# Causal attention in a four-part block: probability transposes, values and output projection each one step later, with four probability buffers

## The chip, the core and the metric

The kernel runs on one core of one Trainium2 chip. The metric is the device time of one execution in microseconds (us). The core has five engines that work side by side and wait for each other only through semaphores: TensorE (PE in the rows; its weight loads are PEld), VectorE (DVE), ScalarE (ACT), GpSimd (POOL) and SyncE (SP), which issues the transfers. Each engine runs its own instructions in their order.

## What is computed

The reference runs four stages on x of shape (4, 256, 256): windowed attention, a quantized feed-forward, a selective scan, and then a block of causal attention followed by a mixture of 32 experts. The change lies in the causal attention alone, which is this part of the reference (here 4 sequences of 256 positions, 32 query heads, 4 key and value heads of width 128):

```python
q = (h @ Wq).reshape(B, S, NH, HD)
k = (h @ Wk).reshape(B, S, KVH, HD)
v = (h @ Wv).reshape(B, S, KVH, HD)
q = _rope(q, pos)
k = _rope(k, pos)
...
scores = jnp.einsum('bqhd,bkhd->bhqk', q, k) / jnp.sqrt(jnp.float32(HD))
scores = jnp.where(causal[None, None], scores, jnp.float32(-1000000000.0))
attn = jax.nn.softmax(scores, axis=-1)
o = jnp.einsum('bhqk,bkhd->bqhd', attn, v).reshape(B, S, NH * HD) @ Wo
x = resid + o
```

## The kernel before

Five functions run one after the other: `windowed_attention`, `quantized_ffn`, `selective_scan`, `causal_attention`, `experts`. In `causal_attention` the outermost loop runs over the 4 groups of heads `g` (one key and value head, 8 query heads each), inside it over the 4 sequences `b`, and inside that over the 8 heads of the group. One **step** `n` is one head of one sequence, so a group has 32 steps and the stage 128. A **batch** in this text is the 8 steps of one `(g, b)`, and `r = n % 8` is a step's place in it. All precise products are three matmuls on a high and a low part (`product`, lines 73 to 75).

One head s goes through these pieces of work, each on several engines:

- `scores`: PE multiplies q and k into one of two PSUM banks (`SCOREB[s % 2]`, lines 1534 and 73 to 75). It waits for `exp_done` of head s-2, which has used that bank.
- `peak`: DVE adds the mask (line 1428) and takes two row maxima (line 1432).
- `softmax`: ACT takes the exponential (line 1318), DVE inverts the sums (`rden`, line 1443), POOL multiplies `prob` by them (line 1372) and signals `p_normed`.
- `turn_probs`: PE transposes `prob` in three pieces (line 1544), ACT copies the result (`pt_1`, `pt_h`, lines 1324 and 1325), DVE makes the low part `pt_l` (line 1438) and signals `p_lo`. PE's transpose of head s waits for `p_normed` of s and for `p_lo` of s-1, since there is one bank for it.
- `values`: PE multiplies with v (lines 73 to 75 and 1554), ACT copies `ot_h` (line 1329), DVE makes `ot_l` (line 1447).
- `project_out`: PE multiplies with the output weights (lines 73 to 75); after a batch's last head DVE adds the sum to `z` (line 1457).

Beside the heads, the next batch is prepared: `kv` and `q` project keys, values and queries (PE), rotate them (DVE lines 1389 and 1392, then POOL into `kr` and `qr`, lines 1365 and 1358), and `turn_k`, `turn_q` transpose them (PE lines 1524 and 1514, ACT lines 1301 to 1307, DVE lines 1416 and 1421). There is one `qr` buffer for each half of the positions, and POOL's `q(m, i)` waits until PE has turned all of head quartet m-1. During the first three groups `weights` splits the next group's weights in 9 pieces at every second step (ACT line 1290, POOL line 1342).

The order of all this work is written out by hand in `schedule`, and every engine walks the same list and does its own part of each entry. `yield "scores", *at(1)` in step n means the scores of head n+1. So in step n, before the change, PE does the scores of head n+1, the transposes of n-1, the values of n-2 and the projection of n-3. Steps 0 to 2 are written out, then a loop of three passes of 32 steps starts at step 3, and the last group is written out again.

A step in which PE does these four things alone is called **light** here; a step that also has a projection of q or kv is **heavy**.

Of the kernel before, what the change touches and what calls it, by code (L numbers as in the profile page):

```python
# [17 lines left out]
F32 = mybir.dt.float32  # L18
# [3 lines left out]
ALU = mybir.AluOpType  # L22
# [4 lines left out]
P = 128  # L27
# [1088 lines left out]
def causal_attention(core, z, ln1_w, weights_in, consts):  # L1116
# [10 lines left out]
    with scope:  # L1127
# [19 lines left out]
        v_1 = sb("v1_1", [P, 2, HD1], F32)  # L1147
        neg_max = sb("neg_max1", [P, 2, 2], F32)
        sums = sb("sums1", [P, 2, 2], F32)
        rden = sb("rden1", [P, 2, 2], F32)  # L1150
        prob = sb("prob1", [P, 2, BANDS], F32)
        pt_h, pt_l = (sb(f"pt1_{n}", [P, 2, S], F32R) for n in "hl")
        pt_1 = sb("pt1_1", [P, 2, P], F32)
        ot_h, ot_l = (sb(f"ot1_{n}", [P, 2, S], F32R) for n in "hl")
# [46 lines left out]
        def ahead(g, m):  # L1201
            return (g, m) if m < 2 * B else (g + 1, m - 2 * B)
# [15 lines left out]
        def schedule(g, first, end, last):  # L1218


            for n in range(first, end):
                at = lambda k: (g + (n + k) // STEPS, (n + k) % STEPS)
                own = not last or n < STEPS
                (gg, s), more = at(0), own and (not last or n // REP1 + 1 < B)
                b, r = s // REP1, s % REP1
                if own and (not last or n + 1 < STEPS):
                    yield "scores", *at(1)
                if own:
                    yield "softmax", *at(0)
                if own and (not last or n + 1 < STEPS):  # L1230
                    yield "peak", *at(1)
                if n >= 1 and (not last or n < STEPS + 1):
                    yield "turn_probs", *at(-1)
                if own and r in (1, 2):
                    yield "turn_q", gg, 2 * b + 1, r - 1
                if more and r == 4:
                    yield "turn_k", *ahead_b(gg, b + 1)
                if more and r in (5, 6):
                    yield "turn_q", *ahead(gg, 2 * b + 2), r - 5
                if n >= 2 and (not last or n < STEPS + 2):  # L1240
                    yield "values", *at(-2)
                if n >= 3:
                    yield "project_out", *at(-3)
                if more and r == 1:
                    yield "kv", *ahead_b(gg, b + 1)
                if more and r in (2, 3):
                    yield "q", *ahead(gg, 2 * b + 2), r - 2
                if more and r in (6, 7):
                    yield "q", *ahead(gg, 2 * b + 3), r - 6
                if not last and 6 <= s < 6 + 2 * PIECES and s % 2 == 0:  # L1250
                    yield "weights", gg + 1, (s - 6) // 2
# [4 lines left out]
        def run(eng, does):  # L1256


            def all_of(work):
                for kind, *what in work:  # L1260
                    if kind in does:
                        does[kind](*what)

            all_of([*FIRST, *schedule(0, 0, 3, False)])
            with eng.Fori(0, KVH1 - 1) as g:
                all_of(schedule(g, 3, STEPS + 3, False))
            all_of(schedule(KVH1 - 1, 3, STEPS + 3, True))

        with nc.Block() as block:
            @block.sync  # L1270
# [13 lines left out]
            def _(act):  # L1284
# [30 lines left out]
                def softmax(g, s):  # L1315
                    act.wait_ge(max_ready, STEPS * g + (s + 1))
                    for i, cols in enumerate((slice(0, P), slice(P, BANDS))):
                        act.activation(prob[:, s % 2, cols], psum[:, SCOREB[s % 2], cols], ACT.Exp,  # L1318
                                       bias=neg_max[:, s % 2, i:i + 1],
                                       accum_out=sums[:, s % 2, i:i + 1]).then_inc(exp_done, 1)  # L1320

# [12 lines left out]
            @block.gpsimd  # L1334
            def _(pool):
                def weights(g, piece):

                    hi, lo, raw, row, rows, cols = weight_piece(piece)
                    where = ds((g & 1) * raw.shape[1] + row, rows)
                    src = raw[:, row:row + rows, cols]  # L1340
                    pool.wait_ge(w_hi, PIECES * g + (piece + 1))
                    ins = pool.tensor_tensor(lo[:, where, cols], src, f(hi[:, where, cols]), ALU.subtract)
                    if piece in (2 * KD, PIECES - 1):
                        ins.then_inc(w_ready, 1)

                for piece in range(2):
                    weights(0, piece)
                norm.gpsimd(pool)
                for piece in range(2, PIECES):
                    weights(0, piece)  # L1350

                def q(g, m, i):
                    pool.wait_ge(parts, q_index(g, m, i) + 1)
                    before = turn_index(g, m - 1, 1) if m else k_turn_index(g, 0) - 1
                    if not known(before, 0):
                        pool.wait_ge(qk_turned, before + 1)
                    slot = q_index(0, m, i) % 2
                    pool.tensor_tensor(qr[:, i, :], part_a[:, slot, :], part_b[:, slot, :], ALU.add).then_inc(roped, 1)  # L1358

                def kv(g, b):  # L1360
                    index = kv_index(g, b)
                    pool.wait_ge(parts, index + 1)
                    slot = kv_index(0, b) % 2
                    cols = slice(0, 2 * HD1)
                    pool.tensor_tensor(kr[:].rearrange("p t n -> p (t n)"), part_a[:, slot, cols], part_b[:, slot, cols],
                                       ALU.add).then_inc(roped, 1)

                def softmax(g, s):
                    pool.wait_ge(rden_ready, STEPS * g + (s + 1))
                    for i, cols in enumerate((slice(0, P), slice(P, BANDS))):  # L1370
                        at = prob[:, s % 2, cols]
                        ins = pool.tensor_tensor(at, at, rden[:, s % 2, i:i + 1].to_broadcast([P, (i + 1) * P]), ALU.mult)  # L1372
                    ins.then_inc(p_normed, 1)

                run(pool, dict(q=q, kv=kv, softmax=softmax, weights=weights))

            @block.vector
            def _(dve):
# [61 lines left out]

                def softmax(g, s):
                    dve.wait_ge(exp_done, 2 * STEPS * g + (2 * s + 2 + 4))
                    dve.reciprocal(rden[:, s % 2, :], sums[:, s % 2, :]).then_inc(rden_ready, 1)  # L1443

                def values(g, s):
                    dve.wait_ge(o_hi, STEPS * g + (s + 1))
# [17 lines left out]
            def _(pe):  # L1464
# [75 lines left out]
                def turn_probs(g, s):  # L1540
                    pe.wait_ge(p_normed, STEPS * g + (s + 1))
                    pe.wait_ge(p_lo, STEPS * g + (s + 1))
                    for i in range(3):
                        ins = pe.transpose(psum[:, PTURNB, i * P:(i + 1) * P], prob[:, s % 2, i * P:(i + 1) * P],  # L1544
                                           core.ident[:])
                    ins.then_inc(p_turned, 1)

# [373 lines left out]
```

## Time and profile before

| | |
|---|---|
| time before, median of 3 runs | 1260.85 us (1260.09 to 1262.29) |
| profiled execution | 1260.24 us, of which its span is 1258.4 us |
| busy share of the span | PE 88%, DVE 68%, ACT 51%, POOL 50% |
| the causal attention in the span | about 478 to 954 us; heads from 492.6 us |
| in 490 to 954 us | PE busy 431.66 us, DVE 362.16, ACT 281.72, POOL 245.40; mean granted TensorE clock 0.99 |

The span is the time from the first to the last instruction in the trace. Times in rows are microseconds from its start. The granted clock is TensorE's clock as a share of 2.4 GHz, so 0.50 stands for 1.2 GHz. Matmuls are pipelined: the recorded length of one (0.28 us for 128x256) is longer than the distance to the next (0.12 us), so a recorded gap is shorter than the time that PE's queue stood still.

### The profile page before, as it was taken

To read this page: it belongs to the slowest core of one execution; us is meant where nothing else is said; L and a number is where in the kernel's file an instruction comes from. 1 tells how busy PE (TensorE), PEld (TensorE's weight loads), DVE (VectorE), ACT (ScalarE), POOL (GpSimd) and SP (SyncE) were. 2 spreads that over 40 slices of the span, in tenths; PEclk is the share of its full clock that TensorE was granted. 3 is DMA by queue.
4 is the path that set the end of the run, shared out by engine and by line. 5 is a ranking of instruction groups with operands and counts; after the bars stand their busy time and mean duration, and the time that the engine had idled before them with its cause. 6 is when DMAs were issued, how large, how long until landed. Compare 5 with 4: busy or idle time off the path is not lost. (4 is left out here: it accounts for less than half of the span.)

```text
span 1258.4 us, 22579 instructions
## 1 busy us (share of the span) xinstructions
PE 1105.8 (88%) x6776; PEld 916.0 (73%) x6776; DVE 856.1 (68%) x2126; ACT 637.7 (51%) x2027; POOL 623.7 (50%) x648
## 2 busy tenths in 40 slices
PE   5499989597579956999899999999997999999998
PEld 4366656386335525888888888888896888888887
DVE  4766785555388885878778777777886555555555
ACT  4356644122379942666566556655563434333332
POOL 3632361255277762565466446644442455555554
PEclk9699989588789977999999999999997999999999
DMA  8000000000212302002000200000001111111111
GB/s 231 1 1 1 0 0 1 10 1 11 69 67 84 126 11 76 2 2 77 3 1 2 77 3 2 1 2 2 1 2 28 50 50 43 44 50 50 38 50 46
DMA packets 43966, 41.35 MB, mean 33 GB/s; under 512 B 6161, under 2 KB 39985, under 8 KB 43873
## 3 DMA queue, kind: packets, MB, share of 16 engines
q1 hardware_dynamic: 42144, 39.02, 10.1%
q10 hardware_dynamic: 1728, 1.18, 0.3%
q8 instruction: 46, 0.75, 0.3%
q14 instruction: 48, 0.39, 0.1%
HBM read 39.08 MB, written 1.11 MB: 32 GB/s over the span
## 5 line engine op out<-in xcount | busy, mean ns | idle before, releaser
L1732 POOL TENSOR_TENSOR hid_l<-hid,hid_h 128x512 fp32r<-128x512 f32 x66 | 85.6, 1297 | 131.1 <-ACT hid_h L1701 131.1
L1358 POOL TENSOR_TENSOR qr<-r_part_a,r_part_b 128x512 f32<-128x512 f32 x64 | 82.4, 1287 | 125.1 <-DVE r_part_b L1392 123.8
L1372 POOL TENSOR_TENSOR prob<-prob,rden 128x128 f32<-128x128 f32 (+1 forms) x256 | 124.3, 509 | 37.5 <-DVE rden L1443 37.5
L1782 DVE TENSOR_TENSOR hid<-psum,silu 128x512 f32<-128x512 f32 x66 | 45.6, 691 | 129.3 <-ACT silu L1699 129.3
L1318 ACT ACTIVATE prob<-psum,neg_max 128x128 f32<-128x128 f32 (+1 forms) x256 | 106.0, 424 | 36.3 <-DVE neg_max L1432 31.4
L1774 DVE SCALAR_TENSOR_TENSOR x<-psum,weight,x 128x256 f32<-128x256 f32 x264 | 108.8, 475 | 0.0
L73 PE MATMUL psum<-xt_h,gu_l 128*128 128x512 f32 x264 | 105.5, 400 | 2.4 <-POOL gu_l L1717 2.4
L75 PE MATMUL psum<-xt_h,gu_h 128*128 128x512 f32 x264 | 104.5, 396 | 0.0
L74 PE MATMUL psum<-xt_l,gu_h 128*128 128x512 f32 x264 | 104.0, 394 | 0.0
L1699 ACT ACTIVATE silu<-psum 128x512 f32<-128x512 f32 x66 | 39.5, 598 | 117.6 <-PE psum L75 117.6
L913 POOL TENSOR_TENSOR drive<-u,b_all 128x1024 f32<-128x1024 f32 x32 | 76.3, 2387 | 40.1 <-DVE u L1007 20.2
L1324 ACT ACTIVATE pt<-psum 128x128 f32<-128x128 f32 x128 | 36.1, 282 | 115.1 <-PE psum L1544 114.7
L1544 PE MATMUL psum<-ident,prob 128*128 128x128 f32 x384 | 65.2, 279 | 25.8 <-POOL prob L1372 25.8
L1016 DVE TENSOR_TENSOR_SCAN h<-psum,drive 128x512 f32<-128x512 f32 x64 | 76.4, 1214 | 12.7 <-ACT psum L951 12.4
L73 PE MATMUL psum<-wo_h,ot_l 128*128 (+1 forms) x256 | 82.6, 323 | 0.2 <-DVE ot_l L1447 0.2
L1432 DVE TENSOR_REDUCE neg_max<-psum 128x1 f32<-128x128 f32 (+1 forms) x256 | 79.5, 352 | 4.4
L1389 DVE TENSOR_TENSOR r_part_a<-psum,rope 128x512 f32<-128x512 f32 (+1 forms) x80 | 50.7, 634 | 38.7 <-PE psum L75 38.6
L73 PE MATMUL psum<-wd_h,hid_l 128*128 128x256 f32 x264 | 74.7, 283 | 0.6 <-POOL hid_l L1732 0.6
L75 PE MATMUL psum<-wd_h,hid_h 128*128 128x256 f32 x264 | 74.7, 283 | 0.0
L74 PE MATMUL psum<-wd_l,hid_h 128*128 128x256 f32 x264 | 74.6, 282 | 0.0
L1087 PE MATMUL psum<-scaled,ident 128*128 128x512 f32 x128 | 70.9, 637 | 2.4
L74 PE MATMUL psum<-wo_l,ot_h 128*128 (+1 forms) x256 | 72.1, 282 | 0.0
(251 smaller groups left out, 3711.5 us busy)
## 6 DMA issues: line engine op xcount, KB each, us to landing
b_all<-scan_b_rows SPq DMA_DIRECT2D x16, 512.0 KB, 3.6
early<-in_L_ffn_Wq_dram SPq DMA_DIRECT2D x4, 1024.0 KB, 5.4
early<-in_L_ffn_Wo_dram SPq DMA_DIRECT2D x4, 1024.0 KB, 8.3
raw<-in_L_ffn_Wg_dram SPq DMA_DIRECT2D x32, 128.0 KB, 2.2
raw<-in_L_ffn_Wu_dram SPq DMA_DIRECT2D x32, 128.0 KB, 2.2
raw<-in_L_ffn_Wd_dram SPq DMA_DIRECT2D x32, 128.0 KB, 2.3
x<-_attn_hidden_states_dram SPq DMA_DIRECT2D x8, 128.0 KB, 4.6
early<-in_L_ffn_w_up_q_dram SPq DMA_DIRECT2D x1, 1024.0 KB, 6.3
```

Source lines behind the costliest of these rows:

```text
L73: pe.matmul(out, ll, rh, start=start, stop=False, skip_group_check=shared)
L74: pe.matmul(out, lh, rl, start=False, stop=False, skip_group_check=shared)
L75: return pe.matmul(out, lh, rh, start=False, stop=stop, skip_group_check=shared)
L913: pool.tensor_tensor(drive[:, k, :], u[:, k, :], b_all[:, n % BBUF, :], ALU.mult).then_inc(driven, 1)
L1016: dve.tensor_tensor_scan(h[:, k, cols], psum[:, DECAYB + i % 2, :], drive[:, k, cols], 0.0, ALU.mult, ALU.add).then_inc(scanned, 1)
L1087: pe.matmul(psum[:, YB[k] + half, :], core.ident[:], scaled[:, i % 4, :, :], start=n == 0, stop=n == NS - 1, skip_group_check=True).then_i ...
L1318: act.activation(prob[:, s % 2, cols], psum[:, SCOREB[s % 2], cols], ACT.Exp, bias=neg_max[:, s % 2, i:i + 1], accum_out=sums[:, s % 2, i: ...
L1358: pool.tensor_tensor(qr[:, i, :], part_a[:, slot, :], part_b[:, slot, :], ALU.add).then_inc(roped, 1)
L1372: ins = pool.tensor_tensor(at, at, rden[:, s % 2, i:i + 1].to_broadcast([P, (i + 1) * P]), ALU.mult)
L1432: ins = dve.tensor_reduce(neg_max[:, s % 2, i:i + 1], psum[:, SCOREB[s % 2], cols], AX.X, ALU.max, negate=True)
L1732: pool.tensor_tensor(hid_l[:, j, cols], hid[:, c, :], f(hid_h[:, j, cols]), ALU.subtract)\
L1774: dve.scalar_tensor_tensor(core.x[:, t, :], src, scale, core.x[:, t, :], ALU.mult, ALU.add)\
```

## The change

Three things are changed together. The transposes of a head's probabilities are done two steps behind its softmax entry instead of one, values three instead of two, and the output projection four instead of three; the preparation of keys, values and most queries moves one step later with them. `prob` and `rden` have four slots instead of two. The loop starts at step 4 instead of 3. The work itself is the same: each engine issues the same number of compute instructions.

```diff
-        rden = sb("rden1", [P, 2, 2], F32)
-        prob = sb("prob1", [P, 2, BANDS], F32)
+        rden = sb("rden1", [P, 4, 2], F32)
+        prob = sb("prob1", [P, 4, BANDS], F32)
...
-                if n >= 1 and (not last or n < STEPS + 1):
-                    yield "turn_probs", *at(-1)
+                if n >= 2 and (not last or n < STEPS + 2):
+                    yield "turn_probs", *at(-2)
                 if own and r in (1, 2):
                     yield "turn_q", gg, 2 * b + 1, r - 1
-                if more and r == 4:
+                if more and r == 5:
                     yield "turn_k", *ahead_b(gg, b + 1)
-                if more and r in (5, 6):
-                    yield "turn_q", *ahead(gg, 2 * b + 2), r - 5
-                if n >= 2 and (not last or n < STEPS + 2):
-                    yield "values", *at(-2)
-                if n >= 3:
-                    yield "project_out", *at(-3)
-                if more and r == 1:
+                if more and r in (6, 7):
+                    yield "turn_q", *ahead(gg, 2 * b + 2), r - 6
+                if n >= 3 and (not last or n < STEPS + 3):
+                    yield "values", *at(-3)
+                if n >= 4:
+                    yield "project_out", *at(-4)
+                if more and r == 2:
                     yield "kv", *ahead_b(gg, b + 1)
-                if more and r in (2, 3):
-                    yield "q", *ahead(gg, 2 * b + 2), r - 2
+                if more and r in (3, 4):
+                    yield "q", *ahead(gg, 2 * b + 2), r - 3
                 if more and r in (6, 7):
                     yield "q", *ahead(gg, 2 * b + 3), r - 6
...
-            all_of([*FIRST, *schedule(0, 0, 3, False)])
+            all_of([*FIRST, *schedule(0, 0, 4, False)])
             with eng.Fori(0, KVH1 - 1) as g:
-                all_of(schedule(g, 3, STEPS + 3, False))
-            all_of(schedule(KVH1 - 1, 3, STEPS + 3, True))
+                all_of(schedule(g, 4, STEPS + 4, False))
+            all_of(schedule(KVH1 - 1, 4, STEPS + 4, True))
```

The remaining edits replace `s % 2` by `s % 4` where `prob` and `rden` are indexed (ACT's exponential, POOL's multiplication, DVE's inversion, PE's transpose).

The first place is the last step of a batch on PE (r = 7), where `ident,prob` is the transpose of probabilities, `ident,qr` that of queries and `pt` the values. Before:

```order
L1534 MATMUL psum<-k_0,q_0 128x128
L73 MATMUL psum<-k_h,q_l 128x256
L74 MATMUL psum<-k_l,q_h 128x256
L75 MATMUL psum<-k_h,q_h 128x256
L1541 REGISTER_ALU
L1544 MATMUL psum<-ident,prob 128x128 x3
L73 MATMUL psum<-pt_h,v_l 128x256
```

Now:

```order
L1534 MATMUL psum<-k_0,q_0 128x128
L73 MATMUL psum<-k_h,q_l 128x256
L74 MATMUL psum<-k_l,q_h 128x256
L75 MATMUL psum<-k_h,q_h 128x256
L1541 REGISTER_ALU
L1544 MATMUL psum<-ident,prob 128x128 x3
L1514 MATMUL psum<-ident,qr 128x128 x4
L73 MATMUL psum<-pt_h,v_l 128x256
```

The query transpose has moved from r = 5 and 6 to r = 6 and 7, so it now stands in both steps that also project the next queries.

The second place is ACT's queue in a batch during which weights are split, around the copies of v (`v_1`, `v_h`); `wq_h<-early` is a weight piece. Before:

```order
L1310 REGISTER_ALU
L1312 ACTIVATE v_1<-psum 128x128
L1313 ACTIVATE v_h<-psum 128x128
L1316 REGISTER_ALU
L1318 ACTIVATE prob,sums<-psum,neg_max 128x128
L1318 ACTIVATE prob,sums<-psum,neg_max 128x256
L1324 ACTIVATE pt_1<-psum 128x128
```

Now:

```order
L1310 REGISTER_ALU
L1312 ACTIVATE v_1<-psum 128x128
L1313 ACTIVATE v_h<-psum 128x128
L1290 ISA
L1290 ACTIVATE wq_h<-early 128x512
L1316 REGISTER_ALU
L1318 ACTIVATE prob,sums<-psum,neg_max 128x128
L1318 ACTIVATE prob,sums<-psum,neg_max 128x256
```

The kv entry has moved from r = 1 to r = 2, an even step that can also hold a weight piece, so that piece now stands between the copy of v and the next exponential.

The third place is the beginning of the stage on PE, step 1 after its scores (`wkv` is the projection of keys and values). Before:

```order
L1544 MATMUL psum<-ident,prob 128x128 x3
L1514 MATMUL psum<-ident,qr 128x128 x4
L73 MATMUL psum<-wkv_h,xt_l 128x256
L74 MATMUL psum<-wkv_l,xt_h 128x256
L75 MATMUL psum<-wkv_h,xt_h 128x256
```

Now:

```order
L1514 MATMUL psum<-ident,qr 128x128 x4
L1534 MATMUL psum<-k_0,q_0 128x128
L73 MATMUL psum<-k_h,q_l 128x256
L74 MATMUL psum<-k_l,q_h 128x256
L75 MATMUL psum<-k_h,q_h 128x256
L1544 MATMUL psum<-ident,prob 128x128 x3
L1514 MATMUL psum<-ident,qr 128x128 x4
L73 MATMUL psum<-wkv_h,xt_l 128x256
```

Step 1 now holds only one query transpose after its scores; the first probability transpose and the kv projection follow behind the scores of step 2.

## Rows read from the trace of the kernel before

**Rows 1.** The page of the profile: its first line.

```profile
span 1258.4 us, 22579 instructions
```

**Rows 2.** Stretches: length, busy PE, PEld, DVE, ACT, POOL, granted clock, DMA, GB/s.

```profile
518.36:547.19 28.83, 27.21 (x207) 25.56 (x206) 22.79 (x70) 18.71 (x72) 18.38 (x25) 1.00 0.01 1
...
604.81:635.75 30.94, 27.33 (x208) 25.47 (x207) 23.05 (x70) 17.53 (x69) 13.43 (x21) 1.00 0.01 3
...
896.57:925.29 28.72, 27.01 (x208) 25.53 (x206) 22.81 (x70) 17.00 (x68) 13.43 (x21) 1.00 0.01 2
```

**Rows 3.** Waits of PE, 490 to 954 us: total us, times, longest.

```profile
PE psum L1544 <- POOL prob L1372: 25.8, 31, 1.0
```

**Rows 4.** Timeline, 842 to 847 us: start, length, instruction, idle before it and releaser.

```profile
842.88 0.69 DVE L1389 TENSOR_TENSOR r_part_a<-psum,rope 128x512 f32<-128x512 f32 x1 [0.53 <-PE psum L75]
...
844.15 0.15 DVE L1443 RECIPROCAL rden<-sums 128x2 f32<-128x2 f32 x1
...
844.31 1.30 POOL L1358 TENSOR_TENSOR qr<-r_part_a,r_part_b 128x512 f32<-128x512 f32 x1 [1.38 <-DVE r_part_b L1392]
...
844.89 0.38 PE L1534 MATMUL psum<-k,q 128*128 128x128 f32 x2
...
845.21 0.41 DVE L1438 TENSOR_TENSOR pt_l<-psum,pt_h 128x256 fp32r<-128x256 f32 x1
...
845.35 0.28 PE L75 MATMUL psum<-k_h,q_h 128*128 128x256 f32 x1
...
845.56 1.93 POOL L1372 TENSOR_TENSOR prob<-prob,rden 128x128 f32<-128x128 f32 x4
...
846.27 0.17 DVE L1443 RECIPROCAL rden<-sums 128x2 f32<-128x2 f32 x1 [0.32 <-ACT prob L1318]
...
846.60 0.55 PE L1544 MATMUL psum<-ident,prob 128*128 128x128 f32 x3 [0.97 <-POOL prob L1372]
```

**Rows 5.** Timeline of POOL, 681 to 685 us, and PE's wait behind it.

```profile
681.28 1.29 POOL L1358 TENSOR_TENSOR qr<-r_part_a,r_part_b 128x512 f32<-128x512 f32 x1 [2.23 <-DVE r_part_b L1392]
682.54 1.28 POOL L1342 TENSOR_TENSOR wo_l<-early,wo_h 128x512 f32 x1
683.78 0.97 POOL L1372 TENSOR_TENSOR prob<-prob,rden 128x128 f32<-128x128 f32 x2
```

**Rows 6.** Timeline of PE and DVE in the last batch's light steps, 939 to 943 us.

```profile
939.74 0.38 PE L1534 MATMUL psum<-k,q 128*128 128x128 f32 x2
940.61 0.41 DVE L1428 TENSOR_TENSOR psum<-psum,causal 128x256 f32<-128x256 f32 x1
941.94 0.38 PE L1534 MATMUL psum<-k,q 128*128 128x128 f32 x2
942.74 0.41 DVE L1428 TENSOR_TENSOR psum<-psum,causal 128x256 f32<-128x256 f32 x1
```

**Rows 7.** Timeline of a heavy step, 675 to 680 us.

```profile
675.61 0.38 PE L1534 MATMUL psum<-k,q 128*128 128x128 f32 x2
...
676.51 0.60 PE L1514 MATMUL psum<-ident,qr 128*128 128x128 f32 x4
...
678.14 0.70 ACT L1290 ACTIVATE wo_h<-early 128x512 f32 x1
...
679.63 0.38 PE L1534 MATMUL psum<-k,q 128*128 128x128 f32 x2
```

**Rows 8.** The start of the heads: timeline of PE and ACT.

```profile
496.22 0.46 PE L1534 MATMUL psum<-k,q 128*128 128x128 f32 x2 [2.31 <-ACT prob L1318]
...
498.01 0.20 ACT L1318 ACTIVATION_READ_ACCUMULATOR prob<-psum,neg_max 128x1 f32 x1
```

**Rows 9.** Busy time by stretch at the start of the heads.

```profile
491.40:498.10 6.70, 4.04 (x28) 3.41 (x27) 4.60 (x13) 1.72 (x8) 3.52 (x4) 1.00 0.00 0
498.10:501.50 3.40, 3.40 (x19) 3.40 (x18) 1.83 (x7) 1.62 (x9) 0.97 (x2) 0.52 0.00 0
```

**Rows 10.** The end of the stage: timeline of PE.

```profile
952.27 0.38 PE L73 MATMUL psum<-wo_h,ot_l 128*128 128x256 f32 x1 [0.23 <-DVE ot_l L1447]
```

More of the change, by code:

```diff
@@ L1317, in softmax @@
                     for i, cols in enumerate((slice(0, P), slice(P, BANDS))):
-                        act.activation(prob[:, s % 2, cols], psum[:, SCOREB[s % 2], cols], ACT.Exp,
+                        act.activation(prob[:, s % 4, cols], psum[:, SCOREB[s % 2], cols], ACT.Exp,
                                        bias=neg_max[:, s % 2, i:i + 1],
@@ L1370, in softmax @@
                     for i, cols in enumerate((slice(0, P), slice(P, BANDS))):
-                        at = prob[:, s % 2, cols]
-                        ins = pool.tensor_tensor(at, at, rden[:, s % 2, i:i + 1].to_broadcast([P, (i + 1) * P]), ALU.mult)
+                        at = prob[:, s % 4, cols]
+                        ins = pool.tensor_tensor(at, at, rden[:, s % 4, i:i + 1].to_broadcast([P, (i + 1) * P]), ALU.mult)
                     ins.then_inc(p_normed, 1)
@@ L1442, in softmax @@
                     dve.wait_ge(exp_done, 2 * STEPS * g + (2 * s + 2 + 4))
-                    dve.reciprocal(rden[:, s % 2, :], sums[:, s % 2, :]).then_inc(rden_ready, 1)
+                    dve.reciprocal(rden[:, s % 4, :], sums[:, s % 2, :]).then_inc(rden_ready, 1)
                 def values(g, s):
@@ L1543, in turn_probs @@
                     for i in range(3):
-                        ins = pe.transpose(psum[:, PTURNB, i * P:(i + 1) * P], prob[:, s % 2, i * P:(i + 1) * P],
+                        ins = pe.transpose(psum[:, PTURNB, i * P:(i + 1) * P], prob[:, s % 4, i * P:(i + 1) * P],
                                            core.ident[:])
```

## The prediction

> **What bounds the kernel now.** The kernel's span is 1258.4 us [rows 1], and the change touches only the causal attention, where the heads run from 492.6 to about 954 us. I read the stretches first: a batch of eight steps takes 28.83 us and PE is busy for 27.21 of it, DVE for 22.79, ACT for 18.71, POOL for 18.38, at a granted clock of 1.00 [rows 2]. The 14 batches between 518.36 and 925.29 us all look like the first and the last of these rows, except the two in which the loop jumps back (30.94 us is one). So PE sets the pace, its clock is full, and what can be won is the time in which its queue stands still.
>
> Then I read who PE waits for. Of its waits in the stage almost all are one kind: 31 times the transpose of probabilities (line 1544) waits for POOL's multiplication (line 1372), 25.8 us together, 0.83 us each [rows 3]. They are two per batch. The matmuls' recorded ends hide a part: the last scores matmul starts at 845.35, its successor would start 0.12 later at 845.47, and the transpose starts at 846.60 [rows 4]. That is 1.13 us of standing still where the row says 0.97, so each wait costs 0.16 more than its record: 0.99 us on average, 31 x 0.99 = 30.8 us in all.
>
> Why POOL is late is seen in the timeline. In [rows 4] DVE is held by the rotation of q and comes to its inversion at 844.15, POOL then adds `qr` (844.31 to 845.61) and only then multiplies two heads' probabilities in one run, 845.56 to 847.49, 0.97 us each; the first is done at about 846.54, and PE starts 0.06 later. In the other kind a weight piece of 1.28 us stands between `qr` and the multiplication [rows 5]. In both the multiplication comes about 1 us after PE wants it, following a heavy step.
>
> **The change part by part.** *The later transpose.* In step n PE now wants head n-2, which POOL multiplied one step earlier. The shortest step of PE is 941.94 - 939.74 = 2.20 us [rows 6], twice the 1.13 us of the longest lateness. So no wait for `p_normed` is left: -30.8 us.
>
> *What is late next.* The same transpose also waits for `p_lo`, DVE's `pt_l` of the head before, made in DVE's previous step; the change keeps this distance at one step. In [rows 4] `pt_l` starts at 845.21 and is done at 845.62, with 0.06 to wake PE 845.68, where PE could go on at 845.47: 0.21 us of wait, hidden so far behind POOL's. It is there because DVE begins its step only after the rotation, about 1.5 us after PE's. Now this sequence (a heavy step, a light one, then a transpose) occurs at r = 1 and at r = 6. At r = 1 I take 0.21. At r = 6 PE's step before is longer by the key transpose of two pieces (0.2 us by the query transposes of four, which take 0.60 with 0.25 of overlap [rows 7]), which cancels that wait, but DVE has a `k_l` more to do (as large as `pt_l`, so 0.41 us, [rows 4]) before the query transpose may reuse its bank, so 0.1 is taken. Bounds are 0 and 0.5 per place: below, if DVE's late start is made good; above, if one more DVE operation of 0.41 falls before the awaited one. Value 0.31 x 15 batches = +4.7 us (bounds 0 and +15).
>
> *Can DVE and ACT keep up with two light steps in a row?* The loop mask, maxima, exponential, inversion, next mask has a period of 942.74 - 940.61 = 2.13 us, shorter than PE's 2.20 [rows 6]. It just does, so nothing is added; the light steps now adjoin as r = 0, 1, with r = 5 alone.
>
> *Queries turned in the same steps as they are projected.* r = 6 and 7 now last as long as the step of [rows 7], 679.63 - 675.61 = 4.02 us, and r = 1 gives up its projection. The sum of PE's work is the same. One wait is new in place: POOL's `qr` of the quartet projected at r = 6 may only be written when PE has turned the previous quartet, which it now finishes at r = 7. PE ends that transpose 677.11 - 675.61 = 1.5 us after a heavy step's start [rows 7]. The input of `qr` comes at the same time: the rotation starts at 842.88 and the inversion behind it at 844.15, and POOL's `qr` begins at 844.31, 844.31 - 842.68 = 1.6 us after PE's step began [rows 4] (842.68 is 2.21 before the scores at 844.89). So POOL is not held: 0 (upper bound 0.1 us, which its idle 1.38 us in front of `qr` covers).
>
> *The weight piece behind kv.* In 6 of the 16 batches ACT now copies a piece of 0.70 us [rows 7] before the next exponential. That exponential is used by PE's scores two steps later, and the two steps that begin meanwhile are heavy (4.02 us, or 3.6 without a query transpose), while ACT's whole work is 18.71 / 8 = 2.3 us a step [rows 2]. Hidden: 0. Without cover it would cost 6 x 0.70 = 4 us.
>
> *Waits too short for the view of waits.* Where the wait falls at r = 0, the transpose of r = 1 is late as well by some 0.1 us, because POOL then has the two multiplications to catch up on. They go too: -1.2 us (bounds 0 and -2).
>
> *The start.* Step 2's scores wait for the first exponential until 496.22, 2.31 us [rows 8], before and after. But then step 1 holds only one query transpose, so step 3's scores wait for the second exponential, done at 498.21 [rows 8], instead of finding kv in front. PE stands still from about 497.2 to 498.25. That is 1 us more idleness, of which the short wait for POOL that stood in step 1 gives a little back: +0.9 us. This is seen only once, since the stage is entered once. `turn_probs`, `values` and `project_out` are each delayed by a step there, which is 1.62 us of PE work (a light step of 2.20 less its scores of 0.58) pushed to the end.
>
> *The end.* The last head's work is a chain (transpose, copies, values, copies, projection) whose last link already waits for DVE [rows 10]. The 1.62 us pushed back now runs behind the last scores as a third light step, and the last transpose comes after it; from there the same chain of copies and products follows. If the chain hid none of it, the stage would end 1.62 us later after its last scores, which only gives back what was pushed; it hides a little, since DVE and ACT have less to do beside it. Taken: -0.2 us (bounds -1.6, all hidden, and +0.5).
>
> *Four buffers.* `prob` of head s is overwritten by head s+4, whose exponential follows long after the transpose; two slots would not do for the new distance. No wait in the view of waits is ACT waiting for a slot, so the slots themselves bring 0. The loop's two jumps (about 2 us each, [rows 2]) now fall after r = 3 instead of after r = 2, both heavy: 0.
>
> *Sum.* -30.8 + 4.7 - 1.2 + 0.9 - 0.2 = -26.6 us. Against the profiled execution, 1260.24 - 26.6 = 1233.6; the median of the runs is 0.6 above it, so **1234 us**.
>
> **The rivals.**
>
> 1. *DVE takes PE's place.* Its late start after each rotation is not made good, and PE waits for `pt_l`, `q_l` or `ot_l` at four places of a batch (the two steps after each light one, r = 1, 2, 6, 7), 0.25 us each as in [rows 4]. For it: DVE's idle gap in front of its inversion is 0.32 us [rows 4], and the margin of the loop 0.07. Against it: DVE is busy for 22.79 of 28.83 us [rows 2], and of 27 us that is still 84%. It gives 1.0 instead of 0.31 a batch, +10 us: 1244.
>
> 2. *A longer stretch at the low clock.* After a stretch in which PE was busy for 4.04 of 6.70 us, the granted clock is 0.52 for 3.4 us (1.2 GHz instead of 2.4) [rows 9]. The thinner start could bring such a stretch once more, at half rate, so 3.4 / 2 = 1.7 us: 1236. Against it: from 498.25 PE has work without a pause. The Trainium skill (TensorE: Matmul & The Clock Gate, Part 1: The HAM clock gate) says that the clock's default state is throttled and that activity releases it. By that rule a start with less work in it is a risk and the later, denser steps are none; the rows at the start agree with it.
>
> 3. *No change.* Another releaser stands right behind POOL in every one of the 31 waits, and PE waits as long as before. In [rows 4] `p_lo` was ready 0.92 us before `p_normed`, the scores' bank even earlier. For 1260 the residue would have to be 0.99 us at each place, over four times what the row shows.
>
> 4. *Slower: POOL held by PE.* The wait of `qr` on the query transpose at r = 7 becomes real, and behind it stand a weight piece, a multiplication and the next `qr`, for which PE's query transpose at r = 1 waits. POOL has 1.30 + 1.28 + 0.97 + 1.30 = 4.9 us of work there [rows 4, 5] against some 5.5 us until PE asks, a margin of about 0.5. A hold of h us then costs h - 0.5 a batch. It decides at h = 2.3 us, where 1.8 us a batch are lost again; at h = 3 it is 15 x 2.5 = 37 us, and the time 1271. The row arithmetic above says h = 0.
>
> **How the numbers follow.** The forecast has 0.60, with its own range of 1229 (no residue: -4.7) to 1239. DVE taking over 0.22 (1239 to 1248). The low clock 0.05. More gained than the sum, where DVE catches up and the end is cheaper, 0.06 (1226 to 1229). No change 0.03. Slower 0.04. The range 1228 to 1246 leaves out a part of the second case, of the larger gain, and the last two, under 2 in 10. A difference of 0.2%, 2.5 us, is about what a measurement of this kernel can tell from no change. Faster by more: 0.93; within: 0.03; slower: 0.04.
>
> **What would show each step.** In the profile after, PE's waits for POOL's line 1372 should be all but gone (under 2 us), a wait for DVE's line 1438 should appear, 0.1 to 0.3 us at one or two places of a batch, and a batch should last 26.9 us (27.2 or more if rival 1 holds). DVE's share of a batch rises to 84% at the same busy time. POOL's `qr` should begin as soon after its rotation as now. PE's first steps should show a second pause, ending near 498.25, and the stretch after it one low-clock stretch of 3.4 us and not two. Wrong would be: waits of POOL on PE's line 1514, exponentials that PE's line 1534 waits for inside a batch, or a batch of over 28 us.

## The result, and the profile after

| | median us | runs | ratio to before | 95% interval |
|---|---|---|---|---|
| before | 1261.57 | 4 (1260.09 to 1263.23) | | |
| changed kernel | 1244.03 | 4 (1241.27 to 1245.24) | 0.9858 | 0.9836 to 0.9879 |

The change saves 17.5 us where 26.6 were forecast. A second comparison (`after_again` below) gave 1241.57 against 1262.94, a ratio of 0.9835 (0.9813 to 0.9856), so 21.4 us. The profiled execution of the changed kernel took 1245.24 us.

Its page begins:

```profile
span 1243.4 us, 22588 instructions
```

The span is 15.0 us shorter than in [rows 1]. The stretches, with the same columns as [rows 2]: a usual batch early in the stage, the first batch in which the loop jumps back, and a late batch.

```profile
519.92:547.09 27.17, 27.02 (x208) 25.55 (x207) 22.65 (x70) 18.97 (x72) 18.36 (x25) 1.00 0.01 1
601.43:632.35 30.92, 28.80 (x207) 26.89 (x206) 22.77 (x70) 17.32 (x69) 13.41 (x21) 0.94 0.01 4
880.27:907.32 27.05, 26.91 (x208) 25.52 (x207) 22.42 (x70) 16.89 (x68) 13.42 (x21) 1.00 0.00 1
```

The first and the last line answer to the first and the last of [rows 2]: 28.83 us became 27.17 and 28.72 became 27.05, with the busy time of every engine within 0.4 us of before. The middle one answers to the 30.94 of [rows 2], and it has hardly moved: PE's busy time rose from 27.33 to 28.80 and the granted clock is 0.94. So a batch with a jump kept none of the gain in this execution.

The waits of PE from 490 to 940 us are these (waited for, total us, times, longest), all that the view lists:

```profile
PE psum L1534 <- ACT prob L1318: 7.0, 4, 2.3
PE psum L1544 <- DVE pt_l L1438: 1.4, 9, 0.2
PE psum L1514 <- DVE q_l L1416: 1.3, 1, 1.3
PE psum L73 <- DVE ot_l L1447: 0.5, 2, 0.3
```

The 31 waits for POOL of [rows 3] are gone without a rest. The wait for `pt_l` has come, as short as forecast (0.2 at most). The four waits for ACT are two at the start and one at each jump of the loop. The one for `q_l` stands at 491.26 us, ahead of the heads.

Where the gain falls in the heads' part of the stage can be read off the starts of the scores (line 1534) in the timelines. The middle columns are means of three profiles each: before, `before_again` and `buffers_only` (same schedule as before) against the changed kernel, `after_again` and `after_third`. "n = 8" stands for the scores that PE does in step 8, and `z` takes the sum of each batch.

| us | before | changed | difference |
|---|---|---|---|
| first scores to those of n = 8 | 28.34 | 27.74 | -0.6 |
| 14 batches, n = 8 to 120 | 406.80 | 386.57 | -20.2 |
| n = 120 to the last scores | 15.29 | 14.44 | -0.8 |
| last scores to the last sum into `z` | 9.82 | 11.65 | +1.8 |
| together | 460.25 | 440.40 | -19.9 |

The traces' 19.9 us and the timed 17.5 and 21.4 agree. The rest of the program is the same code, and it differs from profile to profile by itself: 304.4 us after `z` in before, 306.0 in the changed kernel.

### The profile page after: what moved, and what is told of

It is laid out like the page before. It is cut to its first block and busy times, and to the rows that moved or that the text cites. A ratio compares the mean times of both kernels' runs of the same rounds, so it can differ in the third digit from the quotient of the medians.

```text
span 1243.4 us, 22588 instructions
## 1 busy us (share of the span) xinstructions
PE 1112.4 (89%) x6776; PEld 922.0 (74%) x6776; DVE 852.4 (69%) x2126; ACT 638.6 (51%) x2027; POOL 622.9 (50%) x648
## 5 line engine op out<-in xcount | busy, mean ns | idle before, releaser
L1080 PEld LDWEIGHTS psum<-ident,h 128*128 128x128 f32 x256 | 32.7, 144 | 54.4 <-issue 27.9
```

## The experiments

Each was timed against the kernel before on the same chip, and each was profiled once. "Heads to `z`" is the time from the first scores to the last sum into `z`, the last line of the table above. A ratio is the time divided by that of before, with its 95% interval. In the edits "..." stands for lines left out, among them the same replacement at other places.

**The change again.** Is the difference of the first comparison stable, and are the batches with a jump always so long?

> The changed kernel once more, nothing edited. Its first profile starts the heads 3.7 us later than the profile of before (496.3 against 492.6 us) and needs 3.4 us more after the last scores, in stages that the change does not touch. Theory A (chance: how many stretches at 1.2 GHz fall into the other stages differs from run to run): this profile differs from the first by 1 to 4 us in the start of the heads or in the experts, the batch stays at 27.15 us, and the median is 1241 to 1245. Rival B (the changed program is systematically slower outside the attention): heads start again at 496 us and the part after the last scores is again 317.6 us, both within 0.5 us.

Median 1241.57 us (1237.42 to 1244.23, 5 runs), ratio 0.9835 (0.9813 to 0.9856); heads to `z` 438.51 us. The two batches with a jump, stretches as above:

```profile
597.12:626.27 29.15, 27.26 (x207) 25.45 (x206) 22.68 (x70) 17.43 (x69) 13.43 (x21) 1.00 0.02 4
707.88:737.38 29.50, 27.27 (x208) 25.47 (x207) 22.68 (x70) 17.43 (x69) 13.41 (x21) 1.00 0.01 4
```

The median is within the 1241 to 1245 that were expected. The heads began at 491.84 us, so the later start of the first profile (496.26) was not the change's, against rival B. The part behind the last scores was again 317.6 us, as rival B had it; 306.0 of it lie behind `z`, and `before_again` below has 306.0 there too, so this isn't the change's either.

The same kernel now passes the jumps at full clock: PE is busy for 27.26 us instead of 28.80, and the batch is 1.8 us shorter. A usual batch is 27.15 us in both, so the jumps cost 4.35 us together here and 7.39 in the first profile. The gain in usual batches is stable, the price of a jump is not.

**Four buffers alone.** The schedule stays that of before.

```diff
-        rden = sb("rden1", [P, 2, 2], F32)
-        prob = sb("prob1", [P, 2, BANDS], F32)
+        rden = sb("rden1", [P, 4, 2], F32)
+        prob = sb("prob1", [P, 4, BANDS], F32)
...
-                        at = prob[:, s % 2, cols]
+                        at = prob[:, s % 4, cols]
```

> The kernel before with four slots of prob and rden, schedule untouched. Theory: no engine waited for a free slot, so 1261, within 0.2% of before, and 31 waits of line 1544 for POOL again, 25 to 26 us. Rival (two slots held ACT or POOL back and the buffers bring part of the gain): 1250 to 1257.

Median 1262.89 us (10 runs), ratio 1.0001 (0.9988 to 1.0013). PE's waits, as in [rows 3]:

```profile
PE psum L1544 <- POOL prob L1372: 25.9, 31, 1.0
```

They are all there. Slots by themselves bring nothing, as forecast.

**Two slots with the new distance.** The changed kernel, with ACT held until the slot is free. Line numbers behind it are higher by 2.

```diff
-        rden = sb("rden1", [P, 4, 2], F32)
-        prob = sb("prob1", [P, 4, BANDS], F32)
+        rden = sb("rden1", [P, 2, 2], F32)
+        prob = sb("prob1", [P, 2, BANDS], F32)
...
                     act.wait_ge(max_ready, STEPS * g + (s + 1))
+                    if not known(STEPS * g + s, 2):
+                        act.wait_ge(p_turned, STEPS * g + (s - 1))
```

> The changed schedule with the two slots of prob and rden that the kernel before has; to stay free of races ACT's exponential of head s waits until PE has transposed head s-2. Theory: the four slots are what makes the later transpose possible. The exponential of step n can then start only after PE's transpose in the same step, up to 1 us later than now in light steps; the row maxima behind it, pt_l and PE's next transpose follow late, 0.7 to 1 us after each light step. That gives back 15 x 2 x 0.8 = 24 us: 1255 to 1268, with PE waiting for DVE's line 1438 or POOL's 1372. Rival (the slots do nothing, the exponential has slack enough): 1240 to 1245.

Median 1277.63 us (4 runs), ratio 1.0109 (1.0084 to 1.0135): slower than before. A batch takes 29.2 us. PE's largest wait from 490 to 970 us, and the timeline of one place (start, length, instruction, idle and releaser):

```profile
PE psum L1546 <- DVE pt_l L1440: 30.6, 51, 1.3
```

```profile
523.70 0.37 ACT L1320 ACTIVATE prob<-psum,neg_max 128x128 f32<-128x128 f32 x1 [1.87 <-PE psum L1546]
...
525.75 0.41 DVE L1440 TENSOR_TENSOR pt_l<-psum,pt_h 128x256 fp32r<-128x256 f32 x1
...
526.31 0.52 PE L1546 MATMUL psum<-ident,prob 128*128 128x128 f32 x3 [0.80 <-DVE pt_l L1440]
```

This is above the 1255 to 1268 that were expected. The exponential of head s waits 1.87 us for the transpose of head s-2, which the new distance puts into the same step. DVE's inversion stands behind the exponential and `pt_l` behind the inversion, and PE's next transpose waits for that. So the new distance is worth some 20 us only with the slots; the slots alone do nothing, and the distance alone costs 14 to 15 us (by the ratio and by the median of before beside it, 1262.49). At its two jumps the clock stays at 1.00, with PE standing still for up to 2.27 us.

**Only the heads' work later.** Transposes of probabilities, values and projection as in the change; keys, values and queries are prepared in the steps of before. The parts of v get four slots, since a value is now used a step longer. The edit is shown against the changed kernel.

```diff
-                if more and r == 5:
+                if more and r == 4:
                     yield "turn_k", *ahead_b(gg, b + 1)
-                if more and r in (6, 7):
-                    yield "turn_q", *ahead(gg, 2 * b + 2), r - 6
+                if more and r in (5, 6):
+                    yield "turn_q", *ahead(gg, 2 * b + 2), r - 5
...
-                if more and r == 2:
+                if more and r == 1:
                     yield "kv", *ahead_b(gg, b + 1)
-                if more and r in (3, 4):
-                    yield "q", *ahead(gg, 2 * b + 2), r - 3
+                if more and r in (2, 3):
+                    yield "q", *ahead(gg, 2 * b + 2), r - 2
```

> Of the change only transposes of probabilities, values and output projection are later; kv, q, turn_k and turn_q stand where they stood before. v has four slots for this, so that kv may stay at r = 1. Theory: the whole gain comes from the later transpose, so a batch of 26.9 to 27.4 us and a time within 3 us of the changed kernel (1241 to 1247). Rival (the later preparation is needed for it, or costs something): a difference of more than 4 us to either side, seen in the batch.

Median 1239.31 us (4 runs), ratio 0.9809 (0.9794 to 0.9824); heads to `z` 436.25 us. Its stretches at the start, of a usual batch and of the first jump:

```profile
494.86:520.26 25.40, 22.79 (x167) 20.91 (x166) 21.22 (x68) 16.45 (x66) 14.40 (x21) 1.00 0.01 1
543.79:570.89 27.10, 26.94 (x208) 25.50 (x207) 22.64 (x70) 18.82 (x72) 18.38 (x25) 1.00 0.01 2
598.05:627.95 29.90, 27.40 (x208) 25.50 (x207) 22.77 (x70) 17.61 (x69) 13.47 (x21) 1.00 0.01 4
```

The median is a little below the 1241 to 1247 that were expected. A usual batch is as long as with the whole change, so the later preparation brings nothing there. At the start it costs 2.3 us (27.74 against 25.40), and PE keeps its full clock here. The clock stays at 1.00 at its jumps too, which cost 5.1 us together above two usual batches: the time is spread over two or three steps instead of one.

**The loop written out.** The three passes are unrolled in the program.

```diff
-            with eng.Fori(0, KVH1 - 1) as g:
+            for g in range(KVH1 - 1):
```

> The changed kernel with the loop over three groups written out, so that no engine jumps. In its trace the two batches with a jump last 30.9 and 30.8 us instead of 27.15: a pause of about 2 us and a stretch of 3.4 us at 1.2 GHz after each. Theory: both vanish with the jump, 2 x 3.7 = 7.4 us less, 1236 to 1237 and no stretch at 1.2 GHz between 510 and 920 us. Rival A (only the pause goes, the clock falls anyway somewhere): 1240. Rival B (fetching a longer program costs as much as the jumps): 1243 or more.

Median 1236.81 us (5 runs), ratio 0.9795 (0.9781 to 0.9808); heads to `z` 432.91 us. Two stretches of it:

```profile
500.00:510.00 10.00, 9.14 (x58) 8.72 (x59) 7.44 (x26) 6.67 (x29) 3.60 (x7) 0.83 0.00 1
510.00:910.00 400.00, 397.75 (x3045) 377.15 (x3044) 332.44 (x1036) 264.64 (x1036) 233.19 (x339) 1.00 0.04 13
```

Without jumps the clock stays at 1.00 from 510 to 910 us, and PE is recorded busy for 99.4% of it. The stretch of low clock at the start (0.83 over these 10 us) is still there; it belongs to the start and not to the loop. This is the forecast of this run, 1236 to 1237 and no low clock in the batches. The 14 batches take 379.21 us against 386.57 with the loop: the two jumps cost 7.4 us on average, of which 6.5 stand in their own batches.

**The loop of the kernel before written out.** The same edit on before.

> The kernel before with its loop written out. Its two jumps cost 2.1 and 1.6 us in the profile, with no stretch at 1.2 GHz behind them. Theory (the fall of the clock behind a jump is new with the change, in some of its runs): 3.7 us less, 1258 to 1260, so less than the 4.8 us that unrolling takes off the changed kernel. Rival (the clock falls behind jumps in some runs of the kernel before as well): 5 us less or more, 1257.5 or below.

Median 1257.36 us (10 runs), ratio 0.9964 (0.9950 to 0.9978); the 14 batches take 402.88 us against 406.80. So the jumps of the kernel before cost 3.9 us by the traces and 4.5 (2.8 to 6.3) by the times. The changed kernel pays 7.4 by the traces, and 4.8 by the medians of `unrolled` and `after_again`, so the times don't settle whether it pays more. The median lies where the rival had it (1257.5 or below), but the interval of the gain, 2.8 to 6.3 us, holds the theory's 3.7 as well. Without jumps on either side the 14 batches went from 402.88 to 379.21 us, 23.7 us less, and heads to `z` from 455.59 to 432.91.

**Both together.** Only the heads' work later, and the loop written out.

> The kernel with only the heads' later transposes, values and projection (preparation as before, four slots of v), with the loop written out. heads_only was 2.3 us below the changed kernel; unrolling took 4.8 us off the changed kernel. If both add up: 1234 to 1236. If heads_only's gain is the jump's (its jumps cost 2.8 and 2.3 us without a fall of the clock): 1236.8, as unrolled.

Median 1234.31 us (5 runs), ratio 0.9773 (0.9755 to 0.9792); heads to `z` 429.77 us, no stretch at low clock at the start of the heads or in the batches. Heads' time is 30.5 us less than the mean of before, but some 4 us of that is what before's own jumps cost. Against `unrolled_before` (455.59) it is 25.8 us: that is what the later transposes give without jumps on either side and without the side cost at the start.

**DVE's low part before the next maxima.** The changed kernel, `peak` moved behind `turn_probs`, so that DVE makes `pt_l` first.

```diff
-                if own and (not last or n + 1 < STEPS):
-                    yield "peak", *at(1)
                 if n >= 2 and (not last or n < STEPS + 2):
                     yield "turn_probs", *at(-2)
+                if own and (not last or n + 1 < STEPS):
+                    yield "peak", *at(1)
```

> The changed kernel with DVE's mask and maxima of the next head put behind its pt_l instead of before it (PE, ACT and POOL queues unchanged). In the changed kernel PE's transpose after each light step waits for pt_l: a step r = 1 lasts 2.97 instead of 2.64 us and r = 6 4.22 instead of 4.05. Theory: what is left of the wait is DVE's order after the late rotation; with pt_l first it vanishes, 15 x 0.5 = 7 us less, 1234 to 1236, batch 26.65 us. Rival (the maxima and exponentials get late instead, and DVE waits for pt_h): the batch stays above 27.1 us or grows, 1242 or more.

Median 1254.30 us (4 runs), ratio 0.9925 (0.9896 to 0.9954), 8 to 13 us worse than the change (by the ratios and by the medians of its two comparisons), where 1234 to 1236 was the theory. DVE's two largest waits from 490 to 955 us:

```profile
DVE rden L1443 <- ACT prob L1318: 27.5, 59, 1.4
DVE pt_l L1438 <- ACT pt_h L1325: 22.6, 67, 2.0
```

DVE now stands in front of `pt_l` 67 times until ACT has copied the transpose, with the next head's mask and maxima behind it. The loop from maxima to exponential to inversion is now the longer one, as the rival had it: usual batches are 27.6 to 27.8 us. The wait for `pt_l` can't be removed in this way.

**The same only where DVE has room.** `heads_only_unrolled` with `peak` behind `turn_probs` at r = 0 and r = 4 alone.

```diff
-                if own and (not last or n + 1 < STEPS):
+                if r not in (0, 4) and own and (not last or n + 1 < STEPS):
                     yield "peak", *at(1)
                 if n >= 2 and (not last or n < STEPS + 2):
                     yield "turn_probs", *at(-2)
+                if r in (0, 4) and own and (not last or n + 1 < STEPS):
+                    yield "peak", *at(1)
```

> The kernel with only the heads' work later and the loop written out (heads_only_unrolled, 1234.3), and in the two light steps that follow a rotation (r = 0 and r = 4) DVE's pt_l stands before its mask and maxima. There pt_h has long been copied when DVE comes to it, unlike in the other steps, where putting pt_l first cost 12 us. Theory: PE's wait in the next step (r = 1 lasts 4.38 instead of 4.07, r = 5 2.75 instead of 2.64) goes, and part of it comes back one step later because the maxima are 0.35 us later: 1230 to 1234. Rival: all of it or more comes back: 1234 to 1240.

Median 1232.78 us (5 runs), ratio 0.9763 (0.9749 to 0.9778), the lowest of all. But the heads to `z` took 430.75 us, not less than the 429.77 without the edit: the step r = 1 became 0.2 us shorter (4.38 to 4.16), r = 5 longer by 0.2 (2.75 to 2.94), and the end 1.1 us longer. Its interval overlaps that of `heads_only_unrolled`, and its profile shows no gain in the heads as a whole, so it is not shown to be better.

**The kernel before once more, and the changed one once more.** What does before do at the start and the jumps in another execution, and does the low clock behind the jumps come back?

> The kernel before once more, for a second profile. In the first, the heads begin at 492.6 us and 304.4 us follow after the last sum into z; seven profiles of other versions have 491.8 to 496.3 and 306.0 to 308.5 there, with 17 to 24 us at 1.2 GHz behind the attention. Theory: the first profile of before was a short one in the stages that the change does not touch, by chance; this one has 306 us or more after z, and its execution takes 1261 to 1264. Rival: those stages are always shorter with the kernel before, 304.4 us again.

Median 1262.28 us (12 runs), ratio 0.9994 (0.9978 to 1.0010), as it should be for the same code. The profiled execution was one of 1256.58 us, below what was expected of it, because its heads began at 489.07 instead of 492.58; after `z` it took 306.0 us. Heads to `z` took 459.60. The batch with the first jump:

```profile
599.76:630.25 30.49, 27.27 (x207) 25.45 (x206) 23.06 (x70) 17.54 (x69) 13.44 (x21) 1.00 0.01 3
```

> The changed kernel a third time, for a third profile. Theory: the fall of the clock behind each of the two jumps (3.4 us at 1.2 GHz, seen in the first profile and not in the second) comes and goes by chance, so the two batches with a jump last 29.1 to 29.5 us without it and 30.8 to 30.9 with it, and nothing between; the other batches are 27.05 to 27.2 us.

One run of 1243.72 us. The two jumps:

```profile
599.56:630.58 31.02, 28.77 (x207) 26.92 (x206) 22.79 (x70) 17.32 (x69) 13.42 (x21) 0.94 0.01 4
712.09:743.12 31.03, 28.80 (x207) 26.92 (x206) 22.78 (x70) 17.32 (x69) 13.42 (x21) 0.95 0.02 4
```

So two of three profiles of the changed kernel have a low clock behind both jumps, and both times these batches last 30.8 to 31.0 us. Of the other kernels with the new schedule and the loop, `peak_after` has the low clock behind both and `two_slots` behind none. None of the three of the old schedule has one, `before_again`'s 1.00 above among them, nor the one of `heads_only`.

## Why the prediction was off by 10 us, and right in its main mechanism

**The waits for POOL: right.** All 31 went, and nothing took their place at that size. In usual batches the trace gives the size as well. Steps of the changed kernel last, for r = 0 to 7 (medians): 2.20, 2.97, 4.07, 3.62, 3.61, 2.43, 4.22 and 4.04 us. Rival 3 (no change) is refuted, and so is rival 4 (slower, POOL held by PE): POOL's `qr` starts straight behind the rotation, and PE's query transposes wait for nothing inside the batches. The waits that went were a little larger than forecast: where a light step stood in a batch of before with such a wait it lasted 3.23 us instead of 2.20, so 1.03 for the 0.99 taken.

**What is late next: right place, too small.** PE waits for `pt_l` at r = 1 and r = 6. The timeline of the changed kernel at such an r = 1:

```profile
524.15 0.69 DVE L1389 TENSOR_TENSOR r_part_a<-psum,rope 128x512 f32<-128x512 f32 x1 [0.64 <-PE psum L75]
...
525.42 0.15 DVE L1443 RECIPROCAL rden<-sums 128x2 f32<-128x2 f32 x1
...
526.48 0.41 DVE L1438 TENSOR_TENSOR pt_l<-psum,pt_h 128x256 fp32r<-128x256 f32 x1
526.61 0.28 PE L75 MATMUL psum<-k_h,q_h 128*128 128x256 f32 x1
526.83 0.98 POOL L1372 TENSOR_TENSOR prob<-prob,rden 128x128 f32<-128x128 f32 x2
527.04 0.52 PE L1544 MATMUL psum<-ident,prob 128*128 128x128 f32 x3 [0.15 <-DVE pt_l L1438]
```

PE could have gone on at 526.61 + 0.12 = 526.73 and started at 527.04: it stood still for 0.31 us. `pt_l` ended at 526.89, 0.16 behind that, and PE needed 0.15 more to start. It is 0.15 in each of the 15 waits of this kind in this profile (the view above counts the nine longest), and 0.06 (0.054 to 0.056) in each of the 31 waits for POOL in before. The prediction had taken 0.06 for both, from a wait for POOL in [rows 4]. POOL's multiplication seen here is of the next head, which no longer matters. By the lengths of the steps the wait is 0.33 us at r = 1 (2.97 against 2.64) and 0.17 at r = 6 (4.22 against 4.05): 0.50 a batch for the 0.31 forecast. On the other side the short waits at r = 1 that went were 0.18 (4.21 against 4.03 before), where 0.08 was taken. The forecast's terms for a batch are -1.98 - 0.08 + 0.31 = -1.75 us, measured is 28.80 - 27.15 = 1.65 (the "26.9" that the prediction gives for a batch was rounded too low; its own terms give 27.05). Over 14 batches that is 1.4 us. So rival 1, DVE taking PE's place at 1.0 a batch, isn't what happened, although its time of 1244 is the one measured.

**The loop's jumps: put at nothing, wrongly.** "The loop's two jumps (about 2 us each, [rows 2]) now fall after r = 3 instead of after r = 2, both heavy: 0." By the profiles they cost 2.8 us more (the times above leave it open): 6.5 us above two usual batches as a mean of three profiles, instead of 3.7. A jump of the changed kernel in the timeline, on ACT, POOL and PE:

```profile
619.42 0.37 ACT L1318 ACTIVATE prob<-psum,neg_max 128x128 f32<-128x128 f32 x1 [2.55 <-issue]
...
620.06 1.28 POOL L1358 TENSOR_TENSOR qr<-r_part_a,r_part_b 128x512 f32<-128x512 f32 x1 [1.92 <-DVE r_part_b L1392]
...
620.44 0.48 PE L1534 MATMUL psum<-k,q 128*128 128x128 f32 x2 [1.95 <-ACT prob L1318]
```

ACT stands for 2.55 us with nothing to wait for that the profile shows, its instructions come late; PE waits behind its exponential. The Trainium skill (Runtime: NRT & Kernel Launch, Instruction fetch mechanics) says that a taken branch whose target isn't in the window already loaded makes the engine fetch it by DMA before it goes on. The trace agrees: these are all transfers of the 4.3 us around the jump (queue, packets, MB, share of the DMA engines).

```profile
q8 instruction: 2, 0.03, 3.7%
q14 instruction: 3, 0.02, 2.0%
```

Five packets in 4.3 us, where the 43 us from 547 to 590 have eight; from 510 to 910 us the changed kernel loads 63 such packets and `unrolled` 46. The trace does not name the fetch as what ACT stands for; but in `unrolled`, ACT never stands for over 1 us with nothing to wait for between 590 and 760 us. What comes behind the jump is in the stretches:

```profile
617.00:621.30 4.30, 2.35 (x14) 1.72 (x13) 2.98 (x8) 0.91 (x4) 2.38 (x4) 1.00 0.06 13
621.30:624.70 3.40, 3.40 (x16) 3.27 (x15) 1.93 (x6) 1.74 (x7) 1.01 (x3) 0.50 0.02 5
```

PE was busy for 2.35 of 4.30 us, and then it was granted 0.50, 1.2 GHz, for 3.40 us, in which it does what takes 1.7 at 2.4 GHz. With this fall the jumps cost 7.4 and 7.8 us, without it (`after_again`) 4.35. So 0.7 of the extra belongs to the jump itself and 3.0 to 3.4 to the clock. PE's pause is a little longer too: 1.73 to 2.08 us at the six jumps of the changed kernel, 1.22 to 1.74 at the six of the old schedule, while ACT stands for 2.2 to 2.6 and for 2.1 to 2.4 us; why PE loses more of it is not shown. That the two profiles with the fall are slower for it is shown. That the change made the fall likelier is only suggested: two of three profiles, against none of three, are few, and `heads_only` and `two_slots` jump at the same step without it. Nor does PE's work around the pause tell the cases apart: in the 4.3 us around it PE was busy for 2.22 us at the second jump of `after_again`, without a fall, and for 2.24 at that of `after_third`, with one. This stays open.

**The start: the pause right, rival 2 in part.** Rival 2 had 0.05. The second pause came as forecast. It ends at 502.03 us, 5.77 behind the first scores, where 498.25 and so 5.67 was said:

```profile
502.03 0.77 PE L1534 MATMUL psum<-k,q 128*128 128x128 f32 x2 [0.87 <-ACT prob L1318]
```

One stretch of 3.4 us at half clock follows, not two. That is no more than the profile of [rows 9] had, but it is more than before usually has. Every profile of a kernel with the later preparation (the changed one three times, `unrolled`, `two_slots`, `peak_after`) has this stretch, some 5.5 us behind its first scores. Of the four of the old schedule only the first has it, and the three with the early preparation and late heads have none. The changed kernel's start, as stretch from the first scores to those of n = 8:

```profile
496.26:523.96 27.70, 24.41 (x168) 22.56 (x167) 21.38 (x68) 16.46 (x66) 14.89 (x21) 0.94 0.00 1
```

In the 6.7 us that end 5.5 us behind the first scores (the first stretch of [rows 9] and its like), PE was busy for 3.8 us with the later preparation, 4.0 with the old schedule and 4.4 with late heads alone. The Trainium skill's sentence that was weighed there (TensorE: Matmul & The Clock Gate, Part 1: The HAM clock gate) speaks of a throttled default that activity releases, and the traces lean the same way: the start with least work always fell to 0.50, the one with most kept 1.00. Why the old schedule's, at the same busy time, fell once in four profiles is not shown.

The working erred in reading [rows 9] as what before always does. That profile took 29.38 us up to n = 8; the others of the old schedule took 27.81, 27.84 and, with the loop written out, 27.63. Against these, one more stretch is 3.4 / 2 = 1.7 us; against the mean of the table, in which one of three has it, 1.1.

**The end: nearly right.** The last scores' tail grew by 1.83 us where 1.62 - 0.2 = 1.42 was forecast: the chain hid nothing, and 0.2 us came on top of the 1.62.

**Buffers, the weight piece, POOL's `qr`: right at 0.** `buffers_only` is 1.0001, and none of these shows a wait in the batches.

**Together.** For the 14 batches the terms give -24.5 and the traces -20.2 us: 1.4 from the terms of a usual batch, 2.8 from the jumps. For start and end they give -2.1 and the traces +0.4: 1.1 for the clock at the start, 0.4 at the end, 1.0 not placed. That makes -19.9 for -26.6. That is 6.7 of the 10 us. The rest is not in the heads: the sum starts from an execution of 1260.24 us where the median of before came out at 1261.57, and the times of the first comparison differ by 17.5 us where the traces give 19.9. The untouched stages vary by as much from one execution to the next. So the time fell outside the 1229 to 1239 that had 0.60, into the band that had been given to rival 1 with 0.22; that it is rival 1's very time is chance.

## What to carry to other kernels

Where one engine's queue stands still for a result that another makes one step earlier, taking it a step later and giving it the slots to live in are one change: the slots alone brought nothing, the distance alone cost 14 to 15 us, both together saved some 20. Move only the work that waits; the preparation moved along with it brought nothing in the batches and cost 2.3 us at the start. When the pause at a loop's jump or at a stage's start sits beside TensorE's clock, cost it from several profiles, since one shows only one of its two outcomes.

## What the runs showed of the hardware

- A backward jump of a loop with this large a body stopped ACT for 2.1 to 2.6 us with the kernel before and the changed one, three profiles each (2.55 in the timeline shown); the loop's two jumps cost 3.7 to 7.8 us a kernel by the traces, and writing out the loop gave back 0.36% (before) and some 0.4% (changed).
- A pause of 2 us at a jump can be followed by 3.4 us at 1.2 GHz, in some executions of the same code and not in others: with it the two jumps cost 7.4 and 7.8 us, without it 4.35.
- PE's transpose started 0.15 us behind the end of the DVE operation that it waited for (15 waits), and 0.06 behind that of POOL's (31 waits).
- Stages with the same code differed between profiles: 304.4 to 308.5 us behind the attention, and 489.1 to 496.3 us in front of its heads.
